# Moving two sine products of each half body from GpSimd to VectorE in a one-core transformer kernel

## The chip, the cores and the metric

The kernel runs on one core of one Trainium2 chip. The metric is the device time of one execution in microseconds (us), and the kernel before is given by the median of three runs. The engines are TensorE (PE, with its weight loads as PEld), VectorE (DVE), ScalarE (ACT), GpSimd (POOL, called "the pool" here) and SyncE (SP), which issues the DMAs.

## What is computed

The input is `x` of 4 sequences x 512 tokens x 128 features. A pre-norm global attention with a distance bias comes first, then a stack of six layers on its normed output. Each layer is a local attention (16 heads of 64, windows of 32 tokens that look one window back) and a gated feed-forward part, both with a residual:

```python
def attn_layer(x, Wqkv, qs, ksc, Wo):
    q, k, v = (sh(t) for t in jnp.split(x @ Wqkv, 3, -1))
    q = l2norm(q) * qs
    k = l2norm(k) * ksc
    q = q * cos * scale + rotate_half(q) * sin * scale
    k = k * cos * inv + rotate_half(k) * sin * inv
    return local_attention(q, k, v) @ Wo

for i in range(6):
    x = attn_layer(shift_tokens(x), ...) + x
    x = ffn_layer(shift_tokens(x), ...) + x
```

The change lies in `rotate_half(q) * sin * scale` and its counterpart for `k`, below "the sine products".

## The kernel before

**Bodies and halves.** The six layers take the time from about 424 us to the end. They run as 24 bodies (one layer and one sequence each, `g = 4 * layer + s`), and each body as two halves, `a = 0` and `a = 1`, with 8 heads each. A half holds four head pairs, `i = 0..3`; `m` counts head pairs through the whole kernel. Every engine has its order written out by hand in its own `body`. In half `n` the kernel does the attention of half `n` and, between its pieces, already projects and rotates the q and k of half `n + 1`. The feed-forward part of an earlier body is cut into pieces that are placed in the same way: at `a = 1` the pieces `mean`, `var`, norm and the first three products (`g0`, `g1`, `g2`) of body `g - 1`; at `a = 0` the last products (`v0`, `v1`, `v2`), `down` and the residual of body `g - 2`.

**One head pair.** PE projects q and k into the two banks of `ring0` (L693 to L695, six matmuls). `rope` on VectorE then does two things: a stream shuffle of `ring0` into `swapped` (L1486, neighbours exchanged), and the product of `ring0` with the cosine table into `rot` (L1489, which signals `s_cos`). The projection of the next pair waits for that `s_cos`, as there is one `ring0`. ScalarE squares `swapped` (L1212, `s_sq`), for the norms; only then may `swapped` be overwritten with its product with the sine table. After that the pool adds it to `rot` (L598, `s_rot`).

**Who does the sine product before.** For pairs 0 and 1 the pool does it, in `add` (L592, followed by the add at L598). For pairs 2 and 3 VectorE does it, in `sines` (L1497), both after `rope` of pair 3. There are two `swapped` buffers, so `rope` of pair `m` waits for the add of pair `m - 2`.

**The order on VectorE in a half.** `final(c=1)` (L1503), `rope` 0, [a=1: `centre`, L1528], `maxima` 0 (L1510), `rope` 1, `maxima` 1, [a=0: `p0`, L1547], `rope` 2, [a=0: `p1`; a=1: norm, L1533, L1536 and L1538], [a=0: `p2`], `rope` 3, `sines` 2, `sines` 3, [a=0: residual, L1554], `final(c=0)`, [a=0: `mid`, L1520 to L1524].

**The order on PE in a half.** Project 0, values (L901), [`v0` or `mean`], scores for the maxima u=0 (L912, L923), project 1, scores u=1, values, project 2, turn of the maxima (L936, waits for both `maxima`), [`v1`, which waits for `p0`; or `var`, L1009], turned scores e=0 (L945, L952), [`v2`], norms of squares (L878), project 3, turned scores e=1, values, [`down`, L1028; or `g0`, which waits for the last norm step L1538], norms of squares (L878), [half of the output projection, L997; or `g1`], values, attend e=0 (L980), sums (L966), [L997; or `g2`], attend e=1.

**The order on the pool in a half.** [a=0: two splits of the shifted input], add 0, [s=1, a=1: `split_w1`, L622 and L624; s=2, a=1: `scale_tables`, L630], add 1, `scale_out` (L605, two multiplies), add 2, add 3. In the bodies with s=3 each add is followed by `split_pair` (L574 and L579, four small operations).

Of the kernel before, what the change touches and what calls it, by code (L numbers as in the profile page):

```python
# [10 lines left out]
ALU = mybir.AluOpType  # L11
# [4 lines left out]
SEQS, TOK, D = 4, 512, 128  # L16
# [4 lines left out]
GROUP = 4  # L21
# [11 lines left out]
PAIRS = INNER // P  # L33
# [98 lines left out]
def build_program(nc, x, w_kqv, m, w_qkv, q_scale, k_scale, w_o, ln_g, ln_b, w_1, b_1, w_2, b_2,  # L132
                  rotary, masks, blocks, wide, out):
    with ExitStack() as ctx:
        def sb(name, shape, dt=F32):
            return ctx.enter_context(nc.sbuf_tensor(name, shape, dt))

        def sem(name):
            return ctx.enter_context(nc.semaphore(name))
# [24 lines left out]
        tab_sb = sb("tab_sb", [P, 2 * 4 * TOK])  # L164
# [95 lines left out]
        s_tab = sem("tables_scaled")  # L260
# [33 lines left out]
        s_p = sem("qk_projected")  # L294
        s_sq = sem("qk_squared")
        s_sw = sem("halves_swapped")
        s_sin = sem("first_swapped_times_sin")
        s_sin2 = sem("last_swapped_times_sin")
        s_cos = sem("qk_times_cos")
        s_rot = sem("qk_rotated")  # L300
        s_n2 = sem("norm2")
# [81 lines left out]
        def some(value):  # L383
            return not (isinstance(value, int) and value <= 0)
# [180 lines left out]
        def _(pool):  # L565
# [16 lines left out]

            def add(m, par, i):
                part, dst = swapped[m % 2][:], rot[:, par, i, :, :]
                done = 2 * (m // GROUP) + i % 2 + 1
                if i < 2:
                    l = m // (PAIRS * SEQS)
                    at = (l % 2) * 4 * TOK + 2 * TOK
                    if m % (PAIRS * SEQS) == 0:
                        pool.wait_ge(s_tab, l + 1)  # L590
                    pool.wait_ge(s_sq, m + 1)
                    pool.tensor_tensor(part, part, tab_sb[:, at:at + 2 * TOK].rearrange("p (i t) -> p i t", i=2), ALU.mult  # L592
                                       ).then_inc(s_sin, 1)
                    pool.wait_ge(s_sin, done)
                else:
                    pool.wait_ge(s_sin2, done)
                pool.wait_ge(s_cos, m + 1)
                pool.tensor_tensor(dst, dst, part, ALU.add).then_inc(s_rot, 1)  # L598

# [34 lines left out]
            def body(l, s, par, first, last):  # L634
                g = SEQS * l + s
                for a in range(2):
                    n = 2 * g + a
                    nxt = not (last and s == SEQS - 1 and a == 1)
                    if a == 0 and not (last and s == SEQS - 1):
                        shifted_parts(g + 1, (s + 1) % SEQS)  # L640
                    for i in range(4):
                        if nxt:
                            add(4 * n + 4 + i, 1 - a, i)
                        if s == SEQS - 1 and not last:
                            pool.wait_ge(s_p, PAIRS * g + 4 * a + i + 1)
                            split_pair(l + 1, 4 * a + i)
                        if i == 1 and not (first and s == 0 and a == 0):
                            scale_out(n - 1, g, 1 - a)
                        if s == 1 and a == 1 and i == 0:
                            split_w1(l, 1 - par)  # L650
                        if s == 2 and a == 1 and i == 0 and not last:
                            scale_tables(l + 1, 1 - par)
# [21 lines left out]
            for i in range(4):  # L674
                add(i, 0, i)
# [13 lines left out]
        def _(pe):  # L689
# [297 lines left out]
            def ffn_parts(f):  # L987
# [36 lines left out]
                def down():  # L1024
                    pe.wait_ge(f_he, 2 * NF * (f + 1))
                    pe.wait_ge(s_w2, 32 * (l + 1))
                    for j, (_, n) in enumerate(FFN_TILES):
                        mm = pe.matmul(F_BANK[:], w2_sb[0:n, j, :], gates[0:n, j, :], start=(j == 0),  # L1028
                                       stop=(j == NF - 1))
                    mm.then_inc(f_w2, 1)  # L1030
# [319 lines left out]
        def _(dve):  # L1350
# [124 lines left out]
            def rope(g, a, i):  # L1475
                n = 2 * g + a
                m = 4 * n + i
                l = g // SEQS
                if a == 0 and i == 0:
                    dve.wait_ge(s_tab, l + 1)  # L1480
                dve.wait_ge(s_p, m + 1)
                if some(m - 1):
                    dve.wait_ge(s_rot, m - 1)
                at = (l % 2) * 4 * TOK
                both = ring[0][:].rearrange("p a t -> p (a t)")
                dve.stream_shuffle(swapped[m % 2][:].rearrange("p a t -> p (a t)"), both, SWAP).then_inc(s_sw, 1)  # L1486
                if i == 0 and some(n - 1):
                    dve.wait_ge(s_st, 2 * n - 2)
                dve.tensor_tensor(rot[:, a, i, :, :].rearrange("p a t -> p (a t)"), both,  # L1489
                                  tab_sb[:, at:at + 2 * TOK], ALU.mult).then_inc(s_cos, 1)  # L1490

            def sines(g, a, i):
                m = 8 * g + 4 * a + i
                at = ((g // SEQS) % 2) * 4 * TOK
                part = swapped[m % 2][:].rearrange("p a t -> p (a t)")
                dve.wait_ge(s_sq, m + 1)
                dve.tensor_tensor(part, part, tab_sb[:, at + 2 * TOK:at + 4 * TOK], ALU.mult).then_inc(s_sin2, 1)  # L1497

            def final(n, a, c):
                dve.wait_ge(s_rb[c], 32 * (n + 1))  # L1500
                dve.wait_ge(s_rot, 4 * n + 2 * c + 2)
                dst = rot[:, a, 2 * c:2 * c + 2, :, :].rearrange("p g i t -> p (g i) t")
                dve.scalar_tensor_tensor(out=dst, in0=r_all[:, c, :, :], scalar=NORM_CAP, in1=dst, op0=ALU.min, op1=ALU.mult  # L1503
                                         ).then_inc(s_fin, 1)

            def maxima(n, u):
                if u == 0 and some(n):
                    dve.wait_ge(s_tm, n)
                dve.wait_ge(s_s, 2 * n + u + 1)
                dve.tensor_reduce(neg_max[:, 16 * u:16 * (u + 1)],  # L1510
                                  ring[1 + u][:].rearrange("p h (g k) -> p (h g) k", k=2 * WINDOW),
                                  AX_X, ALU.max, negate=True).then_inc(s_mx, 1)
# [51 lines left out]
            def body(g, new=True, old=True, last=False):  # L1564
                mine = ffn_parts(g - 1) if new else {}
                late = ffn_parts(g - 2) if old else {}
                for a in range(2):
                    n = 2 * g + a
                    end = last and a == 1
                    gn, an = (g, 1) if a == 0 else (g + 1, 0)  # L1570

                    def step(first, second):
                        (late.get(first, nothing) if a == 0 else mine.get(second, nothing))()

                    final(n, a, 1)
                    if not end:
                        rope(gn, an, 0)
                    step("", "centre")
                    maxima(n, 0)
                    if not end:  # L1580
                        rope(gn, an, 1)
                    maxima(n, 1)
                    step("p0", "")
                    if not end:
                        rope(gn, an, 2)
                    step("p1", "norm")
                    step("p2", "")
                    if not end:
                        rope(gn, an, 3)
                        sines(gn, an, 2)  # L1590
                        sines(gn, an, 3)
                    step("residual", "")
                    if not end:
                        final(n + 1, 1 - a, 0)
                    if a == 0:
                        mine.get("mid", nothing)()
# [5 lines left out]
            dve.memset(x_shift[HALF:P, :, 0:1], 0.0).then_inc(f_x, 1)  # L1602
            for i in range(4):
                rope(0, 0, i)
            sines(0, 0, 2)
            sines(0, 0, 3)
            final(0, 0, 0)
            body(0, new=False, old=False)
            body(1, old=False)
            for g in range(2, BODIES - 1):  # L1610
                body(g)
# [34 lines left out]
```

## Time and profile before

| | |
|---|---|
| median of three runs | 2367.95 us (2356.84, 2367.95, 2391.07) |
| the profiled execution | 2352.53 us |
| its span on the core | 2350.7 us |
| mean granted TensorE clock | 0.903 of full speed |
| busy: PE, PEld | 1931.9 us (82%), 1141.7 us (49%) |
| busy: DVE, ACT, POOL | 1346.9 us (57%), 1023.3 us (44%), 1278.9 us (54%) |

In the rows a line such as `L1510 DVE` names the source line and the engine. `out<-in` are tiles, then come the shapes. "idle before" in square brackets is how long the engine stood idle ahead of an instruction, and what ended that. `issue` stands for time in which the engine waited for nothing that the profile shows. Between two neighbouring VectorE instructions the rows overlap by about 0.1 us, so what one adds to a full stretch is its start-to-start time.

### The profile page before, as it was taken

Reading aid. Unit: us, or ns where it says so; the run is one execution under the profiler, and the core shown is the slowest. Engines: PE = TensorE matmul, PEld = TensorE weight load, DVE = VectorE, ACT = ScalarE, POOL = GpSimd, SP = SyncE. Lnnn points to the kernel's source line nnn. Section 1 sums busy time; section 2 is a strip of 40 time slices with the busy share of each in tenths; the row PEclk is TensorE's granted clock in tenths of the full one; section 3 lists DMA queues with packets and bytes.
Section 4 is the critical chain, followed back from the end, with each engine's and each line's share of the span. In section 5 each row is a group of like instructions: output and inputs, shape, how many; then the busy total and the mean of one; then the engine's idle time right before and its main releaser. Section 6 shows DMA issues by size and latency. Waiting matters only on the chain.

```text
span 2350.7 us, 95737 instructions
## 1 busy us (share of the span) xinstructions
PE 1931.9 (82%) x44564; PEld 1141.7 (49%) x44592; DVE 1346.9 (57%) x1486; ACT 1023.3 (44%) x1377; POOL 1278.9 (54%) x729
## 2 busy tenths in 40 slices
PE   1889984788889888987888888889888988898776
PEld 0444442555455545554555545545545555555442
DVE  2454344466656576656656665656566656666632
ACT  0454452444444444444445444535444444444441
POOL 3332214555776566665657755757565567556430
PEclk9997696999899989999998999899899998998996
DMA  4000002435353443443444435344435344434331
GB/s 122 2 2 2 1 2 64 91 83 124 80 116 76 114 99 87 108 103 88 107 94 91 114 73 115 92 96 93 109 80 126 74 110 94 107 81 95 82 73 39
DMA packets 105759, 194.45 MB, mean 83 GB/s; under 512 B 18580, under 2 KB 43538, under 8 KB 98194
## 3 DMA queue, kind: packets, MB, share of 16 engines
q1 hardware_dynamic: 105362, 188.32, 35.1%
q8 instruction: 351, 5.75, 1.1%
q14 instruction: 46, 0.38, 0.1%
HBM read 177.55 MB, written 4.46 MB: 77 GB/s over the span
## 4 chain that ended last, share of the span: by engine, by line
PE 62%; DVE 13%; issue 12%; DMA 6%; ACT 5%; SPq 1%; POOL 1%; ACTq 0%; DVEq 0%; POOLq 0%
PE bank L997 6%; PE bank L901 6%; PE ring L980 6%; PE ring L693 5%; DVE swapped L1486 4%; PE ring L695 4%; PE bank L878 4%; PE ring L694 4%; DMA r_all<-r_rows 3%; PE bank L1028 3%; DVE rot L1489 3%; PE ring L952 3%; PE bank L797 2%; PE bank L693 2%; DVE y_parts L1536 2%
## 5 line engine op out<-in xcount | busy, mean ns | idle before, releaser
L598 POOL TENSOR_TENSOR rot<-rot,swapped 128x1024 f32<-128x1024 f32 x192 | 529.8, 2767 | 122.7 <-DVE swapped L1497 115.2
L592 POOL TENSOR_TENSOR swapped<-swapped,tab_sb 128x1024 f32<-128x1024 f32 x96 | 228.4, 2379 | 556.2 <-DVE rot L1489 543.0
L1503 DVE SCALAR_TENSOR_TENSOR rot<-r_all,rot 128x2048 f32<-128x2048 f32 x96 | 236.2, 2461 | 318.7 <-DMA r_all<-r_rows 315.1
L1212 ACT ACTIVATE sq<-swapped 128x1024 f32<-128x1024 f32 x192 | 202.3, 1054 | 308.9 <-DVE swapped L1486 308.6
L901 PE MATMUL bank<-wv_sb,x_tok 128*32 128x128 f32 x6144 | 240.5, 296 | 40.8 <-issue 39.2
L605 POOL TENSOR_TENSOR o_feat<-o_feat,inv_all 128x1024 f32<-128x1024 f32 x96 | 242.5, 2547 | 41.5 <-DMA inv_all<-inv_rows 41.5
L1486 DVE STREAM_SHUFFLE swapped<-ring 128x1024 f32<-128x1024 f32 x192 | 253.7, 1321 | 0.1
L980 PE MATMUL ring<-probs,v_sb 32*64 32x64 f32 (+1 forms) x12288 | 173.4, 239 | 89.9 <-issue 89.7
L1489 DVE TENSOR_TENSOR rot<-ring,tab_sb 128x1024 f32<-128x1024 f32 x192 | 231.7, 1207 | 0.0
L901 PEld LDWEIGHTS bank<-wv_sb,x_tok 128*32 128x32 f32 x6144 | 175.4, 118 | 109.8 <-issue 95.5
L693 PE MATMUL ring<-xs_parts,w_hi 128*128 128x512 f32 x384 | 184.5, 481 | 46.9 <-DVE rot L1489 28.9
L980 PEld LDWEIGHTS ring<-probs,v_sb 32*64 32x64 f32 x12288 | 154.7, 137 | 132.6 <-issue 132.2
L1420 DVE TENSOR_REDUCE inv_all<-ring 128x2 f32<-128x256 f32 (+3 forms) x128 | 103.8, 823 | 149.3 <-PE ring L757 148.5
L1286 ACT ACTIVATE o_feat<-ring 128x1024 f32<-128x1024 f32 x96 | 93.1, 1022 | 213.5 <-PE ring L980 213.5
L997 PE MATMUL bank<-o_feat,wo_sb 128*128 128x512 f32 x384 | 177.1, 604 | 1.3 <-DVE state L1554 1.3
L694 PE MATMUL ring<-xs_parts,w_hi 128*128 128x512 f32 x384 | 164.9, 429 | 6.5 <-issue 6.5
L695 PE MATMUL ring<-xs_parts,w_lo 128*128 128x512 f32 x384 | 165.7, 432 | 5.1 <-issue 5.1
L1229 ACT ACTIVATE v_sb<-bank 128x512 f32<-128x512 f32 x192 | 112.8, 588 | 112.1 <-PE bank L901 111.8
L878 PE MATMUL bank<-sq,wide_sb 128*32 128x512 f32 x768 | 111.4, 649 | 50.3 <-ACT v_sb L1229 50.3
L952 PEld LDWEIGHTS ring<-rot 64*32 64x32 f32 x12288 | 128.1, 105 | 47.6 <-issue 47.4
L952 PE MATMUL ring<-rot 64*32 64x64 f32 (+1 forms) x12288 | 143.2, 224 | 4.6 <-issue 4.1
L693 PEld LDWEIGHTS ring<-xs_parts,w_hi 128*128 128x128 f32 x384 | 78.3, 204 | 121.3 <-issue 106.5
(150 smaller groups left out, 3107.4 us busy)
## 6 DMA issues: line engine op xcount, KB each, us to landing
r_all<-r_rows SPq DMA_DIRECT2D x192, 512.0 KB, 6.4
inv_all<-inv_rows SPq DMA_DIRECT2D x96, 512.0 KB, 6.4
tab_sb<-in_rotary SPq DMA_DIRECT2D x6, 1024.0 KB, 8.0
w_raw<-in_L_ffn_Wqkv SPq DMA_DIRECT2D x48, 128.0 KB, 6.6
wv_sb<-in_L_ffn_Wqkv SPq DMA_DIRECT2D x12, 256.0 KB, 7.4
wo_sb<-in_L_ffn_Wo SPq DMA_DIRECT2D x6, 512.0 KB, 7.6
x_tok<-state SPq DMA_DIRECT2D x24, 128.0 KB, 6.4
x_tok<-state SPq DMA_DIRECT2D x24, 127.8 KB, 6.6
```

Of the source, the lines that this page charges most:

```text
L598: pool.tensor_tensor(dst, dst, part, ALU.add).then_inc(s_rot, 1)
L605: pool.tensor_tensor(dst, dst, inv_all[:, :, 2 * u:2 * u + 2, :].rearrange("p q g t -> p g q t"), ALU.mult).then_inc(s_nrm, 1)
L693: pe.matmul(dst, lh, rh, start=True, stop=False)
L694: pe.matmul(dst, lh, rl, start=False, stop=False)
L695: return pe.matmul(dst, ll, rh, start=False, stop=True)
L901: mm = pe.matmul(N_BANK[SLOT * pair:SLOT * (pair + 1), j * P:(j + 1) * P], x_shift[:, par, at:at + WINDOW], wv_sb[:, 4 * a + pair, :], sta ...
L952: mm = pe.matmul(dst[SLOT * pair:SLOT * (pair + 1), h, at:at + wide_], rot[rows, a, pair, 1, at:at + WINDOW], rot[rows, a, pair, 0, at:at ...
L980: mm = pe.matmul(bank[2 + pair][DIM_HEAD * h:DIM_HEAD * (h + 1), at:at + wide_], v_sb[keys, a, col:col + DIM_HEAD], probs[keys, e, h, at:a ...
L997: mm = pe.matmul(F_BANK[:], wo_sb[:, a, :], o_feat[:, a, :], start=(a == 0), stop=(a == PAIRS - 1), skip_group_check=True)
L1486: dve.stream_shuffle(swapped[m % 2][:].rearrange("p a t -> p (a t)"), both, SWAP).then_inc(s_sw, 1)
L1489: dve.tensor_tensor(rot[:, a, i, :, :].rearrange("p a t -> p (a t)"), both, tab_sb[:, at:at + 2 * TOK], ALU.mult).then_inc(s_cos, 1)
L1503: dve.scalar_tensor_tensor(out=dst, in0=r_all[:, c, :, :], scalar=NORM_CAP, in1=dst, op0=ALU.min, op1=ALU.mult).then_inc(s_fin, 1)
```

## The change

The semaphore of the pool's own sine products goes, and all four sine products of a half signal one semaphore, `s_sin`. The pool's `add` no longer multiplies: it waits for `s_sin` and for the cosine product and adds. On VectorE, `sines` of pair 0 now stands between `maxima` 0 and `rope` 1, and `sines` of pair 1 between `maxima` 1 and `p0` (a=0) or `rope` 2 (a=1). In the start-up, `sines` follows `rope` for pairs 0 and 1.

```diff
             def add(m, par, i):
                 part, dst = swapped[m % 2][:], rot[:, par, i, :, :]
-                done = 2 * (m // GROUP) + i % 2 + 1
-                if i < 2:
-                    l = m // (PAIRS * SEQS)
-                    at = (l % 2) * 4 * TOK + 2 * TOK
-                    if m % (PAIRS * SEQS) == 0:
-                        pool.wait_ge(s_tab, l + 1)
-                    pool.wait_ge(s_sq, m + 1)
-                    pool.tensor_tensor(part, part, tab_sb[:, at:at + 2 * TOK].rearrange("p (i t) -> p i t", i=2), ALU.mult
-                                       ).then_inc(s_sin, 1)
-                    pool.wait_ge(s_sin, done)
-                else:
-                    pool.wait_ge(s_sin2, done)
+                pool.wait_ge(s_sin, m + 1)
                 pool.wait_ge(s_cos, m + 1)
                 pool.tensor_tensor(dst, dst, part, ALU.add).then_inc(s_rot, 1)
...
                 dve.wait_ge(s_sq, m + 1)
-                dve.tensor_tensor(part, part, tab_sb[:, at + 2 * TOK:at + 4 * TOK], ALU.mult).then_inc(s_sin2, 1)
+                dve.tensor_tensor(part, part, tab_sb[:, at + 2 * TOK:at + 4 * TOK], ALU.mult).then_inc(s_sin, 1)
...
                     maxima(n, 0)
                     if not end:
+                        sines(gn, an, 0)
+                    if not end:
                         rope(gn, an, 1)
                     maxima(n, 1)
+                    if not end:
+                        sines(gn, an, 1)
                     step("p0", "")
                     if not end:
                         rope(gn, an, 2)
...
             for i in range(4):
                 rope(0, 0, i)
+                if i < 2:
+                    sines(0, 0, i)
             sines(0, 0, 2)
             sines(0, 0, 3)
```

## Rows read from the trace of the kernel before

**Rows 1.** The page: busy time of each engine; the chain that ended last, by engine.
```profile
PE 1931.9 (82%) x44564; PEld 1141.7 (49%) x44592; DVE 1346.9 (57%) x1486; ACT 1023.3 (44%) x1377; POOL 1278.9 (54%) x729
...
PE 62%; DVE 13%; issue 12%; DMA 6%; ACT 5%; SPq 1%; POOL 1%; ACTq 0%; DVEq 0%; POOLq 0%
```

**Rows 2.** The waits, whole run: who waited for whom, us in total, times, longest.
```profile
POOL swapped L592 <- DVE rot L1489: 543.0, 59, 17.4
...
PE bank L878 <- ACT v_sb L1229: 50.3, 27, 2.9
...
PE ring L693 <- DVE rot L1489: 28.9, 47, 1.6
```

**Rows 3.** Instructions by source line: duration ns min/median/max, then first and last start.
```profile
L1497 DVE TENSOR_TENSOR swapped<-swapped,tab_sb x96: 1205/1215/3416, 388.4 to 2243.4; 128x1024 f32<-128x1024 f32 x96
...
L592 POOL TENSOR_TENSOR swapped<-swapped,tab_sb x96: 2345/2382/2401, 373.1 to 2231.3; 128x1024 f32<-128x1024 f32 x96
...
L1538 DVE SCALAR_TENSOR_TENSOR y_parts<-gates,vecs,y_parts x24: 751/2738/2753, 528.1 to 2317.3; 128x512 fp32r<-128x512 f32 x24
```

**Rows 4.** Timeline of VectorE, middle of a half with a=0 (start us, us, instruction).
```profile
1431.34 1.23 DVE L1510 TENSOR_REDUCE neg_max<-ring 128x16 bf16<-128x1024 f32 x1 [0.80 <-PE ring L923]
...
1432.83 1.34 DVE L1486 STREAM_SHUFFLE swapped<-ring 128x1024 f32<-128x1024 f32 x1
...
1435.19 1.21 DVE L1510 TENSOR_REDUCE neg_max<-ring 128x16 bf16<-128x1024 f32 x1
1436.32 0.73 DVE L1547 SCALAR_TENSOR_TENSOR gates<-bank,b_sb,gates 128x512 f32<-128x512 f32 x1
```

**Rows 5.** Timeline of PE, the same stretch: project 2, the turn, v1.
```profile
1435.41 0.47 PE L693 MATMUL ring<-xs_parts,w_hi 128*128 128x512 f32 x1 [0.56 <-DVE rot L1489]
...
1436.98 0.39 PE L936 MATMUL bank<-mask_sb,neg_max 128*8 128x128 bf16 x4
1437.30 0.50 PE L693 MATMUL bank<-y_parts,w_hi 128*128 128x512 f32 x1
```

**Rows 6.** Timeline of VectorE and PE, a half with a=0 and s=3: p0, then v1.
```profile
1272.70 0.76 DVE L1547 SCALAR_TENSOR_TENSOR gates<-bank,b_sb,gates 128x512 f32<-128x512 f32 x1
...
1276.76 0.80 PE L693 MATMUL bank<-y_parts,w_hi 128*128 128x512 f32 x1
```

**Rows 7.** Timeline of VectorE, a half with a=1 and s=1: second maxima, norm chain.
```profile
1472.32 1.21 DVE L1510 TENSOR_REDUCE neg_max<-ring 128x16 bf16<-128x1024 f32 x1
...
1476.98 1.83 DVE L1533 SCALAR_TENSOR_TENSOR gates<-wide_sb,vecs 128x512 f32<-128x512 f32 x1 [0.35 <-ACT wide_sb L1263]
...
1481.38 2.73 DVE L1538 SCALAR_TENSOR_TENSOR y_parts<-gates,vecs,y_parts 128x512 fp32r<-128x512 f32 x1
```

**Rows 8.** Timeline of the pool, the same stretch.
```profile
1470.55 2.38 POOL L598 TENSOR_TENSOR rot<-rot,swapped 128x1024 f32<-128x1024 f32 x1
1472.90 1.31 POOL L622 TENSOR_TENSOR w_hi<-tab_sb,wide_sb 128x682 fp32r<-128x682 f32 x1
1474.30 1.63 POOL L624 TENSOR_TENSOR w_lo<-tab_sb,w_hi 128x682 fp32r<-128x682 f32 x1
```

**Rows 9.** Timeline of VectorE and the pool, norm chain with a=1 and s=0.
```profile
1400.16 0.89 DVE L1533 SCALAR_TENSOR_TENSOR gates<-wide_sb,vecs 128x512 f32<-128x512 f32 x1 [0.34 <-ACT wide_sb L1263]
...
1403.62 2.74 DVE L1538 SCALAR_TENSOR_TENSOR y_parts<-gates,vecs,y_parts 128x512 fp32r<-128x512 f32 x1
...
1398.11 2.39 POOL L598 TENSOR_TENSOR rot<-rot,swapped 128x1024 f32<-128x1024 f32 x1
1400.45 5.37 POOL L605 TENSOR_TENSOR o_feat<-o_feat,inv_all 128x1024 f32<-128x1024 f32 x2
```

**Rows 10.** Timeline of the pool, a half with a=1 and s=2: the tables.
```profile
1552.18 4.04 POOL L630 TENSOR_TENSOR tab_sb<-tab_sb,scales 128x512 f32<-128x512 f32 x4
```

**Rows 11.** Stretches: length, busy us (x instructions) of PE, PEld, DVE, ACT, POOL; clock; DMA.
```profile
1408.50:1411.90 3.40, 1.68 (x10) 0.78 (x11) 2.46 (x3) 2.71 (x5) 2.00 (x1) 0.91 1.06 213
1411.90:1415.40 3.50, 3.50 (x106) 2.37 (x104) 2.91 (x1) 2.14 (x4) 3.50 (x2) 0.60 0.78 178
```

More of the change, by code:

```diff
@@ L296, in build_program @@
         s_sw = sem("halves_swapped")
-        s_sin = sem("first_swapped_times_sin")
-        s_sin2 = sem("last_swapped_times_sin")
+        s_sin = sem("swapped_times_sin")
         s_cos = sem("qk_times_cos")
```

## The prediction

> **What bounds the kernel now.** I read the page first. PE is busy 82% of the span and holds 62% of the chain that ended last; VectorE holds 13% of that chain and the pool 1% [rows 1]. So the pool, which the change relieves, does not set the end, and VectorE, which gets the work, partly does. The waits, read next, say where. The pool's sine product stands idle for 543.0 us ahead of it, 59 times, waiting for VectorE's cosine product: the pool waits for work rather than the other way round. PE in turn waits for VectorE's cosine product 47 times, once in nearly every half, 28.9 us in all, so about 0.6 us each; it has no slack against VectorE at that place. And PE waits 50.3 us (27 times) ahead of the norms of squares for a ScalarE chain that begins with VectorE's `rope` 3 [rows 2]. The timelines, read last, show both places, and they are the two that the change touches: the stretch `maxima` 0 to `rope` 2, and in a=1 the norm chain behind it.
>
> **What is removed.** 96 pool multiplies of 2.38 us [rows 3], 228 us of pool time, 4.76 us per half. I put this at nothing in time. The pool's first add could be earlier only if its inputs were. In the half with a=1 it ran at 1470.55 [rows 8]; under the change it waits for VectorE's sine product, which stands behind `maxima` 0 and ends near 1470.7 (below). The add does not get earlier, and the same holds for the second.
>
> **What is added: the price of one.** The same instruction, `sines` 2 and 3 on VectorE, takes 1.215 us at the median [rows 3], of which some 0.1 us overlaps its neighbour: 1.13 us start to start. 96 of them are 108 us. If none were hidden, the kernel would lose 108 us; if all were, nothing. These are the two ends. Their long case is 3.416 us [rows 3], an instruction that waited 2.2 us; for the new ones I expect that only where the pool is busy, and it is idle at `sines` 0 and mostly at `sines` 1, outside the splits and the tables.
>
> **The half with a=0.** Take the one at 1431 us. `maxima` 0 ends at 1432.57 and `rope` 1 starts at 1432.83, as soon as project 1 is there: 0.26 us of idle time with the wait for PE. `sines` 0 starts at 1432.5 and holds the engine until 1433.6, so `rope` 1 moves by 0.73 us. Its cosine product releases project 2, which PE already waited 0.56 us for [rows 4, 5], so PE moves by the same, 0.7 us. `maxima` 1, which ended at 1436.40, now ends at 1437.1. Then comes `sines` 1, 1.13 us, and only behind it `p0` (0.73 us), whose result `v1` on PE waits for. Before, `p0` ended at 1437.05 and `v1` started at 1437.30 [rows 4, 5]. Now `p0` ends at 1437.05 + 0.73 + 1.13 = 1438.9 and `v1` starts at 1439.1: PE is 1.8 us late. All that follows on PE in this half (turned scores, norms, `down`, output projection, values, attention) is back to back and moves with it; no later wait is long enough in this half to take it back, since `rope` 2, `p1` and `rope` 3 move with PE. Going through the 24 halves with a=0, 14 look like this (1.6 to 2.2 us each, 25 us). In 4 project 1 comes so late that `sines` 0 is hidden and only `sines` 1 shows (1.0 us, 4 us). In 4, all with s=3, PE is itself late: there `p0` ended at 1273.46 and `v1` started only at 1276.76, 3.3 us of cover that takes everything [rows 6]. The first two have no `p0`. Sum: 29 us.
>
> **The half with a=1.** Here PE is moved by 0.7 us in the same way at project 2, but what PE waits for in the end is the norm chain L1533, L1536, L1538 (then `g0`, and `rope` 3, squares, exponentials, values, norms of squares). Its last part takes 0.751 us at best and 2.738 us at the median [rows 3]: in the example with s=0 the chain takes 6.2 us (1400.16 to 1406.36) while the pool runs its add and both multiplies of `scale_out` until 1405.82 [rows 9]. Each of the three ends about 0.3 to 0.6 us after a pool instruction ended: a VectorE operation waits for the pool's running one, and then the pool for it. The Trainium skill (SBUF — State Buffer, Who interferes with whom) says that a VectorE instruction with two SBUF inputs and a GpSimd one that reads SBUF hold a shared port by an exclusive lock, for the whole instruction. By that rule the trace agrees, 2.738 against 0.751 us, and the rule speaks against this change, as it puts 96 more such instructions on VectorE. So the chain ends by the pool's order, not by its own start, and I follow the pool:
> - s=0: the second add started with the pool's own order before and ended at 1400.50, 3.8 us after the end of `maxima` 1. Now `maxima` 1 is 0.7 us later, `sines` 1 takes 1.1, the start of the add 0.1 and the add 2.4: 4.3 us after the old end. The chain ends 0.5 us later. 5 halves, 2.5 us, and 0.6 us for the one without a norm chain.
> - s=1: `maxima` 1 ended at 1473.53 and the chain at 1484.11 [rows 7]. Now the first add runs from 1470.8 to 1473.2, L622 to 1474.5. `sines` 1 is ready at 1474.2, must wait for L622, ends at 1475.6, and holds back L624 (1.63 us [rows 8]) to 1477.2. The second add then ends at 1479.6, the two multiplies at 1482.5 and 1485.1, and the chain, which now waits for three instead of two of them, at 1485.7: 1.6 us later. 6 halves, 9.6 us.
> - s=2: the tables' four operations, 4.04 us [rows 10], lie behind a first add that is no earlier, take `sines` 1 between them and push the second add: 1.2 us later. 6 halves, 7 us.
> - s=3: the splits are short and PE is late itself: 0.2 us, 1 us in all.
>
> Sum: 21 us. The bounds of this term: 0 if `scale_out` happens to take the port after the chain, and 24 x 1.86 = 45 us if both sines are fully exposed.
>
> **The clock.** After the stretch 1408.50 to 1411.90, in which PE was busy 1.68 of 3.40 us, the granted clock fell from 0.91 to 0.60, that is, to 1.2 GHz for most of the next stretch [rows 11]. This follows nearly every norm chain. The change makes PE idle more, never less, so some more work runs at 1.2 GHz. In the second stretch (clock 0.60 over 3.50 us) the work would have taken 0.60 x 3.50 = 2.1 us at full clock, so one such fall costs up to 1.4 us. I count 3 more of them, 4 us; the bounds are 0 and one in each of 47 halves, 66 us.
>
> **The sum.** 29 + 21 + 4 = 54 us. The profiled execution took 2352.5 us (span 2350.7), so it would take 2406.5. The median of the runs is 2367.95, 15.4 us above; on it the forecast is 2422 us, 2.3% slower. About 2% (47 us) is what a measurement of this kernel can tell from no change, and the forecast lies just beyond it.
>
> **The rivals.**
> - *Mostly hidden* (2385 us). The delay of PE is given back later in the half, at waits whose end does not move with PE: the 12% "issue" in the chain [rows 1] may be such. For it: 0.12 x 2351 = 282 us stand there. Against it: they stand before attention, in the same places behind the norms' broadcast, which is itself released by PE. If a third comes back, 54 falls to about 17 to 35 us, within 2%.
> - *The clock falls more* (2455 us). Project 2 would be waited for 1.3 us and `v1` another 1.1 us, close together, in 14 halves. If that is enough to lose the clock there and the norm chain's stall costs one more stretch, 14 + 12 stretches of 1.3 us, 34 us, are added.
> - *The port comes free* (2320 us, faster). With 4.76 us less per half, the pool could be done with `scale_out` before the norm chain starts. Then the chain takes about 2.2 us (three of 0.75 [rows 3]) instead of 6.2, in 17 halves: -68 us, -10 for the clock that isn't lost, +29 for a=0. It decides where `scale_out` ends within 1.5 us of the chain's start; before, it ended 5.66 us after [rows 9]. The adds can't start before their sines, which speaks against it. The Trainium skill (GPSIMD Engine Reference, 4.1 Engine selection) tells to do an elementwise product on VectorE, as GpSimd takes about twice the time. The rows agree (2.382 against 1.215 us [rows 3]); by that rule alone the change should gain.
> - *The change doesn't do what it says*: excluded, as the same 96 products are issued by the other engine.
>
> **How the numbers follow.** The forecast has 0.62, mostly hidden 0.21, the clock 0.12, the free port 0.05. The forecast's own range is 2400 to 2442 us (a=0 between 18 and 32, a=1 between 10 and 35, clock to 10, as the bounds of the terms don't meet). Hidden on the one side and the clock on the other widen it to 2377 to 2455. Slower by over 2% (above 2415): 0.6 of the forecast's cases and all of the clock's, less some for noise, 0.48. Faster by over 2%: 0.03. Within: 0.49.
>
> **What would show it.** In the profile after: VectorE busy about 1346.9 + 117 = 1464 us, the pool about 1050; PE's wait for the cosine product at project 2 doubled, from 28.9 to about 60 us; in a=0 halves a new wait of about 1.1 us of PE ahead of `v1` for L1547's successor; the three norm steps no shorter than before; the pool's idle time moved ahead of its adds. I am wrong if the norm chain's median falls well below 6.2 us, if PE's "issue" time falls by what its waits for VectorE grow, or if the granted clock leaves 0.89 to 0.91.

## The result and the profile after

The changed kernel takes 2418.56 us (median of four runs, 2399.62 to 2431.41) where the kernel before takes 2372.89 us in the runs beside it: a ratio of 1.0224, 95% interval 1.0165 to 1.0283. The forecast was 2422 us. So the change makes the kernel slower; whether by more than 2% the interval leaves open. The ratios here leave out executions more than 1.5% above the fastest of their kernel and the medians keep them, so the two do not divide out exactly. Here the medians differ by 46 us, and the ratio is worth 53. The profiled execution has a span of 2397.8 us, 47.1 us more than before.

The page of the changed kernel, busy times and the chain by engine (the lines moved up by 12, so L1477 is the cosine product, L1485 the sine product, L1498 `maxima`, L1535 `p0`, L681 to L683 a projection):

```profile
PE 1942.2 (81%) x44592; PEld 1140.1 (48%) x44592; DVE 1459.0 (61%) x1582; ACT 1023.5 (43%) x1377; POOL 1068.6 (45%) x633
...
PE 52%; DVE 20%; issue 13%; DMA 7%; ACT 4%; POOL 2%; SPq 2%; DVEq 0%; ACTq 0%; POOLq 0%
```

VectorE has 96 instructions and 112 us more, the pool 96 instructions and 210 us less, and VectorE's share of the chain rose from 13% to 20% while PE's fell from 62% to 52% [rows 1]. The waits of the changed kernel, whole run:

```profile
POOL rot L586 <- DVE swapped L1485: 935.4, 121, 23.9
...
PE ring L681 <- DVE rot L1477: 60.8, 54, 1.7
...
PE bank L681 <- DVE gates L1535: 29.1, 44, 4.7
```

PE's wait for the cosine product went from 28.9 us (47 times) to 60.8 (54 times) [rows 2]; its wait for `p0` and its kind is now 29.1 us (8.4 us in 4 times before). The relieved pool waits 935.4 us for VectorE. One half with a=0 shows both delays; first VectorE, then PE:

```profile
1463.75 1.23 DVE L1498 TENSOR_REDUCE neg_max<-ring 128x16 bf16<-128x1024 f32 x1 [1.38 <-PE ring L911]
1464.89 1.22 DVE L1485 TENSOR_TENSOR swapped<-swapped,tab_sb 128x1024 f32<-128x1024 f32 x1
...
1466.04 1.33 DVE L1474 STREAM_SHUFFLE swapped<-ring 128x1024 f32<-128x1024 f32 x1
...
1468.38 1.21 DVE L1498 TENSOR_REDUCE neg_max<-ring 128x16 bf16<-128x1024 f32 x1
1469.52 1.21 DVE L1485 TENSOR_TENSOR swapped<-swapped,tab_sb 128x1024 f32<-128x1024 f32 x1
1470.65 0.74 DVE L1535 SCALAR_TENSOR_TENSOR gates<-bank,b_sb,gates 128x512 f32<-128x512 f32 x1
```

```profile
1468.61 0.47 PE L681 MATMUL ring<-xs_parts,w_hi 128*128 128x512 f32 x1 [1.35 <-DVE rot L1477]
...
1470.17 0.39 PE L924 MATMUL bank<-mask_sb,neg_max 128*8 128x128 bf16 x4
1471.45 0.50 PE L681 MATMUL bank<-y_parts,w_hi 128*128 128x512 f32 x1 [0.88 <-DVE gates L1535]
```

Project 2 now waits 1.35 us instead of 0.56, and `v1` waits 0.88 us where it had waited for nothing [rows 5]. The sine products take 1.15 and 1.13 us start to start (1464.89 to 1466.04, 1469.52 to 1470.65), as forecast.

In a half with a=1 and s=1 the norm chain, on VectorE, is no faster than before:

```profile
1512.09 2.14 DVE L1521 SCALAR_TENSOR_TENSOR gates<-wide_sb,vecs 128x512 f32<-128x512 f32 x1
1514.27 2.50 DVE L1524 TENSOR_SCALAR y_parts<-gates,vecs 128x512 fp32r<-128x512 f32 x1
1516.80 2.72 DVE L1526 SCALAR_TENSOR_TENSOR y_parts<-gates,vecs,y_parts 128x512 fp32r<-128x512 f32 x1
```

**Where the time of the layers went.** For this and for the experiments I added up the idle time of PE from its instruction records, between the first and the last turn of the maxima (413.2 to 2268.0 us before, 417.3 to 2317.2 after). "Project 2" is the idle time just ahead of it, "v" that ahead of `v1` and `v2`, "chain" that ahead of `g0`, the second norms of squares (in halves with a=1) and the first scores. "Inside" is idle time between instructions of one source line, in which PE waits for nothing that the profile shows. Small rest groups are left out, so the columns do not quite add up to "idle". "Busy" is the length less that. Each row is one execution, and executions of one kernel lie up to 2% apart, so a difference of a few us between two rows is no finding.

```
us              project 2     v   chain   inside    idle    busy   length
before               19.2   0.9    70.7    161.8   273.4  1581.5   1854.9
changed kernel       47.2  20.9    79.5    148.5   318.0  1581.9   1899.9
```

So +28 at project 2, +20 at `v`, +9 in the chain, -13 inside: 45 us. The time in which PE works is the same, and so is its clock. The stretch of the layers, before and then after:

```profile
413.20:2268.00 1854.80, 1579.82 (x40197) 953.91 (x40196) 1148.87 (x1109) 843.01 (x1088) 1142.21 (x609) 0.93 0.43 97
```

```profile
417.30:2317.20 1899.90, 1580.55 (x40197) 952.58 (x40196) 1253.69 (x1202) 843.23 (x1088) 939.74 (x515) 0.93 0.42 95
```

The rest of the difference, 2 us, lies ahead of the layers and behind them. That front part is not fixed: the first turn of the maxima came anywhere from 406 to 451 us after the start in the profiles of this study, though nothing in it was edited but the first half's start-up; the two latest, 448 and 451, belong to experiments 2 and 12. So single profiles are compared here over the layers alone, and times by the ratios of several runs.

### The profile page after: what moved, and what is told of

It reads as the page before. It is cut to its first block, busy times and chain, and to the rows that moved or that the text cites. A ratio compares the mean times of both kernels' runs of the same rounds, so it can differ in the third digit from the quotient of the medians.

```text
span 2397.8 us, 95759 instructions
## 1 busy us (share of the span) xinstructions
PE 1942.2 (81%) x44592; PEld 1140.1 (48%) x44592; DVE 1459.0 (61%) x1582; ACT 1023.5 (43%) x1377; POOL 1068.6 (45%) x633
## 3 DMA queue, kind: packets, MB, share of 16 engines
q8 instruction: 351, 5.75, 1.1%
## 4 chain that ended last, share of the span: by engine, by line
PE 52%; DVE 20%; issue 13%; DMA 7%; ACT 4%; POOL 2%; SPq 2%; DVEq 0%; ACTq 0%; POOLq 0%
PE bank L985 6%; DVE swapped L1474 6%; PE ring L968 5%; PE bank L889 5%; DMA r_all<-r_rows 5%; PE bank L866 4%; DVE swapped L1485 4%; DVE rot L1477 4%; PE ring L681 3%; PE bank L1016 3%; PE bank L785 2%; PE ring L683 2%; PE ring L682 2%; PE ring L940 2%; PE bank L681 2%
## 5 line engine op out<-in xcount | busy, mean ns | idle before, releaser
L586 POOL TENSOR_TENSOR rot<-rot,swapped 128x1024 f32<-128x1024 f32 x192 | 527.1, 2753 | 935.4 <-DVE swapped L1485 935.4
L1491 DVE SCALAR_TENSOR_TENSOR rot<-r_all,rot 128x2048 f32<-128x2048 f32 x96 | 243.5, 2537 | 315.1 <-DMA r_all<-r_rows 300.7
L681 PE MATMUL ring<-xs_parts,w_hi 128*128 128x512 f32 x384 | 184.0, 479 | 81.1 <-DVE rot L1477 60.8
L1485 DVE TENSOR_TENSOR swapped<-swapped,tab_sb 128x1024 f32<-128x1024 f32 x192 | 242.5, 1283 | 0.0
L1477 DVE TENSOR_TENSOR rot<-ring,tab_sb 128x1024 f32<-128x1024 f32 x192 | 231.4, 1205 | 0.0
L683 PE MATMUL ring<-xs_parts,w_lo 128*128 128x512 f32 x384 | 165.9, 432 | 3.8 <-issue 3.8
L681 PEld LDWEIGHTS ring<-xs_parts,w_hi 128*128 128x128 f32 x384 | 78.4, 204 | 156.1 <-issue 143.3
```

The costliest lines, as they stand in the source:

```text
L681: pe.matmul(dst, lh, rh, start=True, stop=False)
L683: return pe.matmul(dst, ll, rh, start=False, stop=True)
```

## The experiments

Each ratio is to the kernel before, run beside it on the same chip. `...` in a diff marks lines left out; the waits on semaphore counts and the start-up that follow from an edit are among them.

**1. The pool's sine products left out.**

```diff
                     pool.wait_ge(s_sq, m + 1)
-                    pool.tensor_tensor(part, part, tab_sb[:, at:at + 2 * TOK].rearrange("p (i t) -> p i t", i=2), ALU.mult
-                                       ).then_inc(s_sin, 1)
-                    pool.wait_ge(s_sin, done)
...
-                pool.tensor_tensor(dst, dst, part, ALU.add).then_inc(s_rot, 1)
+                pool.tensor_tensor(dst, dst, dst if i < 2 else part, ALU.add).then_inc(s_rot, 1)
```

> The kernel before, with the pool's sine product of pairs 0 and 1 left out and nothing in its place (their rotation is left out: the pool adds rot to itself, so that its add keeps its size). It asks what the relief of the pool is worth by itself. Theory (port): the pool's second add ends 2.4 us earlier, at about 1.3 us after the end of maxima 1 instead of 3.8, so in the halves with a=1 the norm chain L1533, L1536, L1538 waits for the two multiplies of scale_out only and ends about 2 us earlier (median length 4.2 us instead of 6.2): 17 halves x 2 us = 34 us less, perhaps 10 more from the clock, about 2330 us beside 2373 for the kernel before. PE's wait for rope's cosine product at project 2 stays near 29 us. Rival (the pool is off the path altogether, 1% of the chain): the same time as before within 5 us, norm chain 6.2 us.

2344.59 us, ratio 0.9925 (0.9883 to 0.9967). The norm chain takes 4.0 us where it took 6.2, as the port theory said, and its last step is down to the bare time:

```profile
L1535 DVE SCALAR_TENSOR_TENSOR y_parts<-gates,vecs,y_parts x24: 750/751/753, 532.5 to 2307.5; 128x512 fp32r<-128x512 f32 x24
```

This is L1538 of before, whose median was 2738 ns [rows 3]. "Chain" fell from 70.7 to 37.5 us. But the layers became only 14 us shorter (1840.8), because "inside" rose from 161.8 to 185.2. So the relief of the pool alone is worth something, 18 us by the ratio, which the prediction had put at nothing; and of 33 us taken from a wait, 23 came back in waits for which the profile names no engine.

**2 and 3. One sine product moved at a time.** In the second experiment pair 0 goes to VectorE and pair 1 stays on the pool; in the third it is the other way round.

```diff
-                if i < 2:
+                if i in (1,):
...
                     maxima(n, 0)
                     if not end:
+                        sines(gn, an, 0)
                         rope(gn, an, 1)
```

> Only the sine product of pair 0 on VectorE, between maxima 0 and rope 1; pair 1 stays on the pool. Theory: rope 1 and project 2 late by 0.7 us in about 38 halves, so PE's wait for the cosine product near 60 us as in the changed kernel, no wait of PE ahead of v1 beyond 0.25 us, norm chain at the same place after maxima 1 (pool multiply and add as before): +0.7 x 38 = +27 us, about 2400 us. Rival (sine 1 ahead of p0 is the whole cost): within 5 us of the kernel before.

```diff
-                if i < 2:
+                if i in (0,):
...
                     maxima(n, 1)
+                    if not end:
+                        sines(gn, an, 1)
                     step("p0", "")
```

> Only the sine product of pair 1 on VectorE, behind maxima 1; pair 0 stays on the pool. Theory: PE's wait at project 2 stays near 29 us; in halves with a=0 p0 is late by 1.1 us and v1 starts about 1.0 us late in 18 of 22 halves, +18 us; in halves with a=1 the pool's second add ends about where it did (3.6 against 3.8 us after maxima 1), +0 to +5 us: in all +18 to +23 us, about 2394 us. Rival (the delay of rope 1 is the whole cost): within 5 us of the kernel before.

Pair 0 alone: 2406.13 us, ratio 1.0172 (1.0107 to 1.0236). Pair 1 alone: 2375.76 us, ratio 1.0068 (1.0031 to 1.0104). Together 1.024, the changed kernel's 1.0224: the two prices add, within the intervals. Each shows its own wait and not the other's:

```
us              project 2     v   chain   inside    idle    busy   length
before               19.2   0.9    70.7    161.8   273.4  1581.5   1854.9
pair 0 moved         50.5   1.7    76.4    163.3   314.9  1579.7   1894.6
pair 1 moved         21.0  18.3    70.6    153.8   283.1  1576.7   1859.8
```

The waits of the second, and then of the third:

```profile
PE ring L692 <- DVE rot L1488: 60.0, 51, 1.7
```

```profile
PE ring L692 <- DVE rot L1488: 28.0, 47, 1.6
```

Pair 0 cost more than its 27 us (41 by the ratio, 40 in the layers): 31 at project 2, 6 in the chain. Pair 1 cost 16 us by the ratio, a little under the 18 to 23 expected and about its wait of 17 us ahead of `v1` and `v2`. In the one profile its layers are only 5 us longer, with 8 us less inside and 5 us less busy.

**4. `p0` ahead of the second sine product.**

```diff
-                    if not end:
-                        sines(gn, an, 1)
                     step("p0", "")
+                    if not end:
+                        sines(gn, an, 1)
```

> The changed kernel with p0 put ahead of the sine product of pair 1. Theory: in halves with a=0 v1 starts 0.95 us earlier in 18 halves than in the changed kernel and rope 2, p1 and v2 have room, so 17 us less than the changed kernel (2419): about 2402 us; PE's wait at project 2 unchanged near 60 us. Rival (rope 2 and what follows is the path, p0 is not): the time of the changed kernel, 2419 us, with the wait of PE moved from v1 to v2 or project 3.

2411.52 us, ratio 1.0233 (1.0179 to 1.0287): no gain, and my theory of a free 17 us is wrong. "v" is 18.5 us (20.9 in the changed kernel), but it now stands at `v2` instead of `v1`: in a half with s=0, `v1` starts 0.3 us after the turn, and `v2` waits 1.1 us for `p1`, which is queued behind `rope` 2, which is queued behind the sine product:

```profile
1382.39 0.46 PE L681 MATMUL bank<-y_parts,w_hi 128*85 128x512 f32 x1 [1.12 <-DVE gates L1535]
```

In such a half `v2` starts 3.2 us after the turn in the kernel before, 4.3 us in the changed kernel and 4.3 us here, so `p0` first saves nothing. The rival was right. I had said that `rope` 2 and `p1` have room; they had none.

**5. `scale_out` after add 3 in the halves with a=1, in the kernel before.**

```diff
-                        if i == 1 and not (first and s == 0 and a == 0):
+                        if i == (3 if a == 1 else 1) and not (first and s == 0 and a == 0):
                             scale_out(n - 1, g, 1 - a)
```

> The kernel before, with one edit on the pool: in halves with a=1 scale_out (L605, two multiplies of 2.4 us) comes after add 3 instead of after add 1. Theory (the norm chain ends by the pool's order): the three steps now find the pool idle after its second add and take 2.1 to 2.5 us instead of 6.2 in halves with s=0 and s=2, 4 to 5 in those with s=1; PE's waits at g0 and at the second norms of squares (57 us in the profile of before) fall by 35 to 50 us. The first experiment showed that part of such a relief comes back as issue time inside PE's blocks (27 us less waiting there, 23 us more issue, 7 us less work at 1.2 GHz), so a gain of 15 to 45 us: 2315 to 2345 beside 2360. Rival (the chain is slow for a reason of its own, not the pool's): steps as long as before, same time within 5 us.

2349.49 us, ratio 0.9913 (0.987 to 0.9955), about 20 us faster than the kernel before. VectorE in a half with a=1:

```profile
1384.89 0.88 DVE L1533 SCALAR_TENSOR_TENSOR gates<-wide_sb,vecs 128x512 f32<-128x512 f32 x1 [0.35 <-ACT wide_sb L1263]
1385.80 0.48 DVE L1536 TENSOR_SCALAR y_parts<-gates,vecs 128x512 fp32r<-128x512 f32 x1
1386.32 0.75 DVE L1538 SCALAR_TENSOR_TENSOR y_parts<-gates,vecs,y_parts 128x512 fp32r<-128x512 f32 x1
```

Three steps in 2.2 us instead of 6.2 [rows 9], by nothing but the pool's order. "Chain" falls from 70.7 to 41.1 us; "inside" gives 7 back (168.4), and the layers are 20 us shorter. The theory holds, at the lower end of its range; the chain kept 4.0 to 5.3 us in the halves with s=1, as expected, and in two of the six with s=2.

**6, 7 and 8. The same edit on the changed kernel, with `p0` first as well, and on the kernel with only pair 1 moved.**

> The changed kernel with the same edit. Theory: VectorE's placement costs 20 us at v1 and 28 us at project 2 whatever the pool does, so it stays 30 to 50 us slower than the kernel before with the same edit. Rival (the change frees the pool, and this pays once scale_out no longer hides it): within 10 us of the kernel before with the same edit, or faster, as the norm chain no longer waits for the pool's own product in the halves with s=1.

> The changed kernel with p0 ahead of the sine product of pair 1 and scale_out after add 3 in halves with a=1. When p0 alone was put first, the wait of 20 us at v1 came back as 18 us at v2, behind rope 2. Theory: the same here, so the time of the changed kernel with scale_out late within 5 us. Rival: v1 and v2 each have some room once the halves start earlier, 10 to 18 us faster than that.

> Only the sine product of pair 1 on VectorE (behind maxima 1), and scale_out after add 3 in halves with a=1. Theory: v1 waits 18 us, project 2 as in the kernel before; norm chain short: between the two runs before it, 5 to 20 us slower than the kernel before with scale_out late. Rival (issue time takes up the wait at v1 altogether, as it seems to when pair 1 alone was moved): as fast as the kernel before with scale_out late.

The changed kernel with it: 2387.9 us, ratio 1.0067 (1.0015 to 1.0119), about 36 us above the fifth kernel by the ratios, inside the theory's 30 to 50. So VectorE's placement keeps most of its price when the norm chain is free, 36 of 53 us, and late `scale_out` takes more from the changed kernel (37 us) than from the kernel before (20). With `p0` first: 2386.08 us, ratio 1.0051 (0.9999 to 1.0102), the same within the 5 us of the theory. With only pair 1 moved: 2350.08 us, ratio 0.993 (0.9888 to 0.9972), 4 us above the fifth by the ratios. That is on the rival's side: the wait ahead of `v1` and `v2` (19.3 us in the table below) costs nothing that the runs can tell. But with intervals of 10 us to either side they do not exclude the theory's 5 to 20 us.

```
us                      project 2     v   chain   inside    idle    busy   length
5: before, late              17.8   1.2    41.1    168.4   259.6  1575.0   1834.7
6: changed, late             40.7  19.7    29.8    181.9   298.2  1571.1   1869.3
7: changed, late, p0         48.2  18.4    29.0    180.1   306.2  1567.7   1873.9
8: pair 1, late              17.6  19.3    23.8    185.9   275.8  1578.9   1854.8
```

(In the single profile of the eighth the layers are 20 us longer than in the fifth. The profile of the fifth is of its fastest execution, that of the eighth of a middling one, and the twelve runs of each do not show that difference.)

**9. Three quarters of the norms' broadcasts left out.** What are the waits inside?

```diff
                 for h in range(2):
-                    sp.dma_start(r_all[DIM_HEAD * h:DIM_HEAD * (h + 1), k, :, :],
-                                 r_rows[k, h:8:2, :].partition_broadcast(DIM_HEAD)).then_inc(s_rb[k], 16)
+                    w = TOK if c < 2 else TOK // 4
+                    sp.dma_start(r_all[DIM_HEAD * h:DIM_HEAD * (h + 1), k, :, 0:w],
+                                 r_rows[k, h:8:2, 0:w].partition_broadcast(DIM_HEAD)).then_inc(s_rb[k], 16)
```

> The kernel before, with three quarters of each broadcast of the norms into r_all left out after the first two (the other columns keep the norms of the first two, so the scaling of those tokens is left out). It asks what PE's waits for nothing that the profile shows (issue, inside its blocks, 162 us between the first and the last turn of the maxima) hang on. Theory: most of them end about 1.4 us after a packet of the instruction queue does, so they are instruction supply, held up while the broadcasts fill the DMA engines; with less to move they fall to about 100 us or less, and the time by 30 to 60 us. Rival (the supply is late whatever else the DMA engines carry): the same sum of waits within 15 us, the same time within 10 us.

2257.43 us, ratio 0.9519 (0.9441 to 0.9597): 113 us faster, about twice the upper end of what I expected. PE's instructions are the same in number and order. "Inside" falls from 161.8 to 99.8 us, idle time in all from 273.4 to 203.5, and the time at 1.2 GHz in the layers falls with them from 273 to 157 us, while PE's busy time falls by 44 us (1581.5 to 1537.8). The attention line, in the kernel before and here (shapes, then busy us and mean ns, then idle time before and its releaser):

```profile
L980 PE MATMUL ring<-probs,v_sb 32*64 32x64 f32 (+1 forms) x12288 | 173.4, 239 | 89.9 <-issue 89.7
```

```profile
L981 PE MATMUL ring<-probs,v_sb 32*64 32x64 f32 (+1 forms) x12288 | 161.5, 233 | 20.0 <-issue 19.9
```

The stretch of the layers here:

```profile
435.10:2176.40 1741.30, 1535.58 (x40198) 926.83 (x40198) 1191.96 (x1109) 843.70 (x1088) 1191.84 (x610) 0.95 0.24 61
```

The mean DMA share of the layers fell from 0.43 to 0.24. So 62 of the 162 us of waits inside hang on the broadcasts, though no instruction of PE waits for one. In the trace of the kernel before, 75 of the 103 gaps of over 1 us in PE's work since 420 us have a packet of the instruction queue ending shortly ahead of the gap's end, most by 1.4 us (the others are mostly the waits at the norms of squares). Of the 64 of these gaps that stand inside a block, 62 end 1.2 to 2.0 us after such a packet, and the packets come only every 6 us or so. I read these waits as the supply of PE's instructions: 351 packets, 5.75 MB, that get through late while a broadcast of 1 MB (two of 512 KB) fills the DMA engines. That the broadcasts make the packets late is argued, not shown. The smaller broadcasts have another effect too: the wait ahead of the first scores falls from 13.4 to 3.0 us.

**10. Splits and tables ahead of add 0**, on top of the fifth.

```diff
                     for i in range(4):
+                        if s == 1 and a == 1 and i == 0:
+                            split_w1(l, 1 - par)
+                        if s == 2 and a == 1 and i == 0 and not last:
+                            scale_tables(l + 1, 1 - par)
                         if nxt:
                             add(4 * n + 4 + i, 1 - a, i)
...
                             scale_out(n - 1, g, 1 - a)
-                        if s == 1 and a == 1 and i == 0:
-                            split_w1(l, 1 - par)
-                        if s == 2 and a == 1 and i == 0 and not last:
-                            scale_tables(l + 1, 1 - par)
```

> The kernel before with scale_out after add 3 in halves with a=1 (as in the fifth experiment), and split_w1 (s=1) and scale_tables (s=2) ahead of add 0 in those halves, where the pool was idle. Theory: the norm chain takes 2.2 us in the halves with s=1 too (4 to 5.3 before) and in all with s=2, 15 to 20 us less waiting at g0 and the norms of squares, half of which comes back as issue time: 5 to 15 us faster than the fifth, 2335 to 2345 us. Rival (all of it comes back, or add 0 late behind the splits delays rope 2): the same as the fifth within 5 us.

2348.11 us, ratio 0.9959 (0.9915 to 1.0003). The norm chain now takes 2.2 to 2.6 us in the halves with s=1 and s=2 too (4.0 to 5.3 with s=1 in the fifth), and "chain" falls to 32.2 us, but "inside" rises to 184.0 and the layers stay at 1836.2 us (1834.7). All of it comes back: the rival was right, as far as the runs tell. The ratio is not told apart from the fifth's, nor quite from 1.

**11. The first sine product ahead of `maxima` 0.** From the changed kernel:

```diff
                         rope(gn, an, 0)
+                        sines(gn, an, 0)
                     step("", "centre")
                     maxima(n, 0)
-                    if not end:
-                        sines(gn, an, 0)
                     if not end:
                         rope(gn, an, 1)
```

> The changed kernel with the sine product of pair 0 right behind rope 0, ahead of maxima 0, instead of behind it. It asks whether the price hangs on the place. Before maxima 0, VectorE waited 0.80 us for PE's scores in the half with a=0 at 1431 us (the square that it needs was ready at 1430.55, rope 0 ended at 1430.55), so 0.8 of its 1.13 us is free there. Theory (what counts is the idle time just ahead): in halves with a=0 project 2 is late by 0.1 us instead of 0.7, its wait falls from 28.7 to 12 to 18 us; in halves with a=1 centre stands there and leaves no room, wait unchanged near 18 us; v1 unchanged near 20 us; in all 10 to 15 us less than the changed kernel, a ratio of about 1.017 to the kernel before. Rival (VectorE's added busy time counts, wherever it stands): ratio 1.022, waits as in the changed kernel.

2375.0 us, ratio 1.0062 (1.0023 to 1.0102). One call moved ahead of `maxima` 0 takes back 38 us, 1.6% of the time, with the same instructions on every engine; the theory had given it 10 to 15. The expectation gave the two kinds of halves each other's waits: of the 47.2 us at project 2 in the changed kernel, 18.5 are in halves with a=0 and 28.7 in those with a=1. Those of a=0 fell to 7.9, as the theory has it; those of a=1 fell too, to 19.4, against it, and the wait at `g0` from 20.0 to 8.4.

The table row for it: project 2 27.3, v 17.1, chain 61.8, inside 156.4, idle 289.6, busy 1578.0, length 1867.5 us. The rival is out: the added busy time is the same here and costs much less. The halves with a=1 had room as well: in the changed kernel VectorE stood idle there for 27 us in all ahead of `centre` and 12 us ahead of `maxima` 0, of which 16 and 6 us are left. One of them, where the sine product ended 2.96 us before `centre` began:

```profile
1412.48 0.69 DVE L1516 TENSOR_TENSOR wide_sb<-gates,bank 128x512 f32<-128x512 f32 x1 [2.96 <-PE bank L993]
```

But idle time is only about half of the 38 us: project 2 lost 20 us of wait, the chain 18. The pool's first add now starts earlier, and in a half with s=1 it is done with both splits when `sines` 1 starts; the norm chain takes 6.1 us in the halves with s=1 instead of 7.4.

**12. Both: the eleventh with `scale_out` late.**

> All four sine products on VectorE, that of pair 0 right behind rope 0 (as in the eleventh experiment), and scale_out after add 3 in halves with a=1 (as in the fifth). Theory: the two effects add, 1.0062 and about -0.012: a ratio of 0.990 to 0.998 to the kernel before, level with the kernel before with scale_out late (0.9913), since 17 us at v1 remain and part of the rest comes back as issue time. Rival (freed of its products, the pool now lets VectorE win): a ratio below 0.985, faster than the fifth experiment.

2376.6 us, ratio 1.0047 (1.0002 to 1.0093), above the range of the theory: the two effects do not add. "Chain" is down to 19.2 us, "inside" up to 188.7, project 2 28.6, v 20.5. Late `scale_out` was worth 37 us on the changed kernel (experiment 6) and nothing that the runs can tell on this one, and the earlier place was worth 38 us without late `scale_out` and 5 with it. So much of what either brings is the same thing, and the price of a place depends on where the pool stands. The fifth has the lowest ratio of the kernels that compute everything; the eighth and tenth are not told apart from it.

## Why the prediction was right, step by step

- *The pool's work is worth nothing when removed.* Right for this change, but for the reason given second: its adds wait for VectorE's sine products. By itself (experiment 1) the removal is worth 18 us. The blunt "the pool does not set the end" was too strong, since its order sets the end of the norm chain (experiment 5).
- *The price of one*, 1.13 us: measured 1.13 to 1.15 us.
- *a=0, project 2 and `v1`*: forecast 0.7 and 1.1 us in the example; measured 0.8 and 0.9. The wait at `v1` and `v2` grew by 20 us in the layers, and 18 x 1.1 had been counted. With 11 us more at project 2 the halves with a=0 lost 31 us, where 29 had been forecast. Experiment 3 shows that this wait is the second sine product's, but experiment 4 that `p0` is not its only customer, and in experiment 8 the runs do not show its 18 us.
- *Project 2 in both kinds of halves*: the wait for the cosine product was to go from 28.9 to about 60 us and went to 60.8. Experiments 2 and 11 tie it to pair 0 and to its place. In the layers the wait grew by 11 us in the halves with a=0 and by 17 in those with a=1.
- *The norm chain*: in the s=1 half `sines` 1 took 1.41 us and L612 (L624 before) 2.50 instead of 1.63, as each waited for the other; the three steps took 2.14, 2.50 and 2.72 us. The chain ended at 1519.5, 11.0 us after the end of `maxima` 1; 1.6 us later than before was forecast, with `maxima` 1 itself 0.7 late, so 0.9 of its own. Over the six halves with s=1 it was 0.5 us on the mean, with s=2 0.85 (0.5 forecast), with s=0 -0.1 (-0.2 forecast), with s=3 0.2. "Chain" in the table grew by 9 us. With the 17 us at project 2 the halves with a=1 lost 26 us, where 21 had been forecast.
- *The clock*: +4 us forecast; the granted share is 0.93 in both, and PE's busy time moved by 0.4 us. The extra stalls are each short, and the rival with the falling clock did not come. That the clock falls after nearly every norm chain was misread: in the kernel before it stood at 1.2 GHz at some time in the 10 us behind 15 of the 24.
- *What was missing*: the waits inside became 13 us shorter. It is what the rival "mostly hidden" would look like, which had 0.21, but it took a quarter of the loss. (That rival's text has a third coming back, which would leave 36 of 54 us; its 17 us and its 2385 are what two thirds would leave.) Whether the added delays shortened these waits stays open: pair 0 alone added 31 us at project 2 and left them at 163. What the profiles do show is a pattern over the kernels with full broadcasts: with "chain" under 45 us, inside is 168 to 189, and with "chain" over 60 it is 148 to 163.
- *The sum*: delays of 57 us came where 50 had been forecast, the clock took nothing of its 4, and 13 us inside came back that the sum did not have. So 54 us came out at 45 in the layers of the profile, and at 46 (medians) to 53 us (2.24%, the ratio) in the runs. The places and the waits were right; that the total came so close is in part luck, as two errors of opposite sign met.

## What to carry to other kernels

A product that moves to a faster engine costs what is queued behind it: price the place by the idle time just ahead of the first instruction that another engine waits for, not by either engine's share of busy time. Where a chain on VectorE takes longer while GpSimd runs (here 6.2 us instead of 2.2), first move GpSimd's work that has time to spare out of its way, before moving work between the two; then price the place again, as the two edits do not add. And expect a stall taken away to come back in part (here 23 of 33 us).

## What was not expected of the hardware

- PE's instruction stream seems to be held up by data transfers: with three quarters of the norms' broadcasts gone (DMA share 0.43 to 0.24 in the layers), PE's waits inside its blocks fell from 162 to 100 us and the kernel took 4.8% less. Stalls removed elsewhere partly came back there (+23 us in experiment 1, +7 in experiment 5, +16 from the fifth to the tenth).
- A three-step VectorE chain of 2.2 us takes 6.2 us beside a running GpSimd, and each step ends 0.3 to 0.6 us after a GpSimd instruction does. This holds for the middle step too, which reads one large tile only: 0.48 us in experiment 5, 2.50 in the half of the changed kernel shown above. The Trainium skill (SBUF — State Buffer, Who interferes with whom) has the shared port of the two engines as an exclusive lock; the traces of experiments 1 and 5 agree, with 0.751 us for the last step against 2.738.
- The time at 1.2 GHz went with the long stalls, not with the short ones: 273 us in the layers before, 157 with the shorter broadcasts, and about as much as before (277) when some 40 stalls of about 1 us were added or grew.
